# One pool of five PSUM banks in a two-block transformer kernel, and the order of work that comes with it

## The reference, cut to what matters

```
# layer 0: 16 heads of 16, tanh-GELU MLP of 1024
g1, g2, s1, s2, h1, h2 = silu(c) @ Wada.T + bada           # per sequence
a = ln(x) * (s1 + 1) + h1
q, k, v = a @ Wqkv.T + bias
q = q / |q| * scale ;  k = k / |k|                          # per head
x = x + (softmax(q k^T + mask) v @ Wproj.T + bproj) * g1
h = gelu((ln(x) * (s2 + 1) + h2) @ Wfc1.T + bfc1)
x = x + (h @ Wfc2.T + bfc2) * g2
# layer 1: 8 query heads of 32 with one key/value head, rotary positions, gated MLP of 1024
a = rms(x) * w1 * (1 + c @ tw1.T)
q, k, v = a @ Wq.T, a @ Wk.T, a @ Wv.T ; rope(q), rope(k)
x = x + softmax(q k^T / sqrt(32)) v @ Wo.T
b = rms(x) * w2 * (1 + c @ tw2.T)
x = x + (silu(b @ Wg.T) * (b @ Wu.T)) @ Wd.T
```

## Time and profile before

| | us |
|---|---|
| median of 3 runs (325.44 to 325.73) | 325.62 |
| the profiled execution | 326.22 |
| its span in the trace | 324.3 |
| PE busy in it | 297.7 |
| DVE busy | 221.0 |
| ACT busy | 205.8 |
| POOL busy | 155.5 |

### The profile page before, as it was taken

How to read it: one execution, slowest core, us unless ns; L and a number is a source line. 1 busy time by engine, 2 the same in 40 slices (tenths; PEclk the granted TensorE clock), 3 DMA queues, 4 the chain that set the end, 5 groups by cost and what they waited for, 6 DMA issues and landing times.

```text
span 324.3 us, 7219 instructions
## 1 busy us (share of the span) xinstructions
PE 297.7 (92%) x2458; PEld 250.5 (77%) x2458; DVE 221.0 (68%) x535; ACT 205.8 (63%) x698; POOL 155.5 (48%) x289
## 2 busy tenths in 40 slices
PE   6999789899879889977998999999999999999986
PEld 6979567668757667756787787889878988898975
DVE  4864996799885797799768567774748863661431
ACT  3553799999987797885899845448654535531210
POOL 3728885778947725895423453642246231320000
PEclk9596987999999999999999999999999999999999
DMA  6997622020000100000000100000000000000000
GB/s 184 250 299 246 217 83 80 32 68 3 0 2 0 68 0 3 3 1 2 0 2 14 55 0 2 0 17 2 18 1 2 0 18 16 3 0 19 16 2 32
DMA packets 14035, 14.28 MB, mean 44 GB/s; under 512 B 1568, under 2 KB 12960, under 8 KB 14000
## 3 DMA queue, kind: packets, MB, share of 16 engines
q1 hardware_dynamic: 14000, 13.83, 14.0%
HBM read 12.76 MB, written 1.06 MB: 43 GB/s over the span
## 4 chain that ended last, share of the span: by engine, by line
PE 64%; DVE 18%; POOL 8%; issue 5%; ACT 2%; DMA 1%; SPq 1%; DVEq 0%; POOLq 0%; ACTq 0%
PE ps_linear L1572 16%; PE ps_hidden L1376 6%; PE ps_hidden L1378 6%; PE ps_hidden L1377 6%; PE ps_probs L1507 5%; DVE z L1264 3%; PE ps_linear L1542 3%; PE ps_output L1523 3%; DVE neg_max L1275 3%; PE ps_scores L1496 2%; PE ps_hidden L1396 2%; PE ps_scores L1406 2%; PE ps_linear L1376 2%; PE ps_scores L1491 2%; PE ps_turn L1412 2%
## 5 line engine op out<-in xcount | busy, mean ns | idle before, releaser
L986 ACT ACTIVATE z<-z,neg_max 128x128 f32<-128x128 f32 x128 | 49.6, 395 | 4.0 <-DVE neg_max L1275 4.0
L826 POOL TENSOR_TENSOR h_lo<-xn,h_hi 128x256 fp32r<-128x256 f32 x32 | 25.0, 783 | 36.7 <-ACT h_hi L950 36.6
L1006 ACT ACTIVATE probsT<-ps_probs 128x512 f32<-128x512 f32 x48 | 28.4, 591 | 16.9 <-PE ps_probs L1507 14.5
L1507 PE MATMUL ps_probs<-ident,z 128*128 128x128 f32 x192 | 30.9, 285 | 3.7 <-ACT probsT L1006 2.3
L1042 ACT ACTIVATE g_a<-ps_hidden 128x256 f32<-128x256 f32 x32 | 12.4, 386 | 32.1 <-PE ps_hidden L1378 31.0
L1572 PE MATMUL ps_linear<-WdT,g_h 128*128 128x256 f32 x128 | 29.4, 383 | 1.3 <-DVE g_h L1347 1.3
L1572 PE MATMUL ps_linear<-Wfc2T,g_h 128*128 128x256 f32 x128 | 29.3, 382 | 1.3 <-DVE g_h L1334 0.8
L880 POOL TENSOR_TENSOR z<-z,row_inv 128x512 f32<-128x512 f32 x16 | 17.1, 1067 | 27.8 <-DVE row_inv L1289 27.7
L1507 PEld LDWEIGHTS ps_probs<-ident,z 128*128 128x128 f32 x192 | 21.6, 142 | 8.0 <-ACT probsT L1006 3.4
L1572 PEld LDWEIGHTS ps_linear<-Wfc2T,g_h 128*128 128x128 f32 x128 | 23.7, 190 | 4.9 <-issue 1.1
L1572 PEld LDWEIGHTS ps_linear<-WdT,g_h 128*128 128x128 f32 x128 | 23.7, 190 | 4.8 <-issue 1.4
(11 more groups left out here) (171 smaller groups left out, 910.7 us busy)
## 6 DMA issues: line engine op xcount, KB each, us to landing
gamma<-gamma_scratch SPq DMA_DIRECT2D x8, 256.0 KB, 3.5
stage<-in_Wada SPq DMA_DIRECT2D x6, 256.0 KB, 4.9
X<-in_x SPq DMA_DIRECT2D x4, 256.0 KB, 3.8
stage<-in_Wqkv SPq DMA_DIRECT2D x4, 256.0 KB, 5.6
Wfc2T<-in_Wfc SPq DMA_DIRECT2D x1, 1024.0 KB, 7.1
stage<-in_Wfc SPq DMA_DIRECT2D x4, 256.0 KB, 3.6
WdT<-in_Wd SPq DMA_DIRECT2D x1, 1024.0 KB, 8.0
stage<-in_Wg SPq DMA_DIRECT2D x4, 256.0 KB, 2.6
```

What stands on the lines that cost most here:

```text
L826: pool.tensor_tensor(h_lo[:, m, :, j * P:(j + 1) * P], h_full[:, m, j, :, :], h_hi[:, m, :, j * P:(j + 1) * P].bitcast(F32), ALU.subtract) ...
L986: ins = act.activation(z[:, d, u, :], z[:, d, u, :], ACT.Exp, bias=neg_max[:, d, u:u + 1], accum_out=head_sum[:, n % 2, t, u, b:b + 1])
L1006: act.activation(probsT[:, G % 2, :, :], bank_of(key)[:, :].rearrange("p (u q) -> p u q", u=4), ACT.Copy).then_inc(is_freed(key)[0], 1)
L1507: ins = pe.transpose(bank[:, u * P:(u + 1) * P], z[:, G % DEEP, u, :], ident[:, :])
```

## The change

The banks `turn`, `linear`, `hidden0`, `hidden1` and `probs` become `shared0` to `shared4`, one list. A step of any of those kinds takes the first bank of that list, and an emptied bank goes to its end. `scores` and `output` stay as they are. The number of banks is the same. Four assumed durations on DVE and POOL are set anew, and so are all the due times. No computation is added, removed or changed; the same steps run on the same engines in another order.

```
--- before.py
+++ after.py
 SLOT, START, DUE_US = 0.0, 0.0, 0.0
-GROUP_US = [-6.5, -554.0]
-ATT_BASE = [-3890.5, -875.0, -147.0, -2073.0, 1326.5, -859.0, 551.0, 1266.0]
+GROUP_US = [121.5, -772.0]
+ATT_BASE = [-4249.5, -1246.0, -1017.5, -1082.5, 2161.5, -634.0, -415.5, 75.0]
...
-BANK_KINDS = {"turn": ["turn"], "linear": ["linear"], "hidden": ["hidden0", "hidden1"],
-              "scores": ["scores"], "probs": ["probs"], "output": ["output"]}
+BANK_KINDS = {"shared": ["shared0", "shared1", "shared2", "shared3", "shared4"], "scores": ["scores"],
+              "output": ["output"]}
 BANKS = [b for kind in BANK_KINDS.values() for b in kind]
+KIND_OF = {b: kind for kind, banks in BANK_KINDS.items() for b in banks}
...
-                + [("modulated", c) for c in mods], "turn", at=a)
+                + [("modulated", c) for c in mods], "shared", at=a)
...
-                add(("qk_sum", n), "DVE", 1.3, [("qk_square", n), ("head_exp",), last_j.get(("qk", j))], at=a)
-                add(("qk_root", n), "Pool", 3.5, [("qk_sum", n)], at=a)
-                add(("qk_scale", n), "DVE", 1.0, [("qk_root", n)], at=a)
+                add(("qk_sum", n), "DVE", 1.45, [("qk_square", n), ("head_exp",), last_j.get(("qk", j))], at=a)
+                add(("qk_root", n), "Pool", 3.3, [("qk_sum", n)], at=a)
+                add(("qk_scale", n), "DVE", 0.75, [("qk_root", n)], at=a)
...
-                add(("qk_low", n), "Pool", 1.75, [("qk_high", n)], at=a)
-                add(("q_turn", n), "PE", 0.53, [("qk_low", n), last_scores], "turn", at=a)
+                add(("qk_low", n), "Pool", 1.9, [("qk_high", n)], at=a)
+                add(("q_turn", n), "PE", 0.53, [("qk_low", n), last_scores], "shared", at=a)
...
-                free[b.rstrip("01")].append(b)
+                free[KIND_OF[b]].append(b)
```

More of the change, by code:

```diff
@@ L89 @@
-MLP_SPAN = [-1198.5, 1936.5]
+    'Wfc1': 1874.5, 'Wg': 7279.0, 'Wkv': 1646.0, 'Wq': 6943.5, 'Wqkv': 3242.5, 'Wu': -1435.0, 'ada': 2378.0,
+    'tw1': -52.5, 'tw2': -1582.0}
+MLP_SPAN = [-1696.5, 2329.0]
 SHIFT = {
-    'warm': 900.0, 'angles': -2187.5, 'attn_copy': 408.5, 'cond_silu': 2646.0, 'cond_tanh': 268.5, 'down':
-    1119.0, 'exp': 3337.0, 'fc1': -2109.0, 'gamma_load': -3710.0, 'gamma_store': 470.5, 'gate': 868.5,
-    'gate_up': 2067.0, 'gelu': -2310.0, 'gelu_in': 1778.5, 'gelu_inner': 2225.5, 'head_clip': -1104.0,
-    'head_exp': 166.0, 'inv_copy': 1919.0, 'inv_spread': 370.0, 'inv_turn': -492.5, 'k_copy': 120.0,
-    'k_turn': 698.5, 'load': -1753.5, 'load_small': -943.0, 'load_whole': 1820.0, 'load_x': -2746.5,
-    'mask_add': -1389.5, 'modulate': 4259.0, 'modulated': -3996.0, 'norm_apply': -4120.5, 'norm_high':
-    -993.0, 'norm_low': 3131.5, 'norm_mod': 1463.0, 'norm_probs': -802.5, 'norm_root': 7283.0, 'norm_stats':
-    -4034.5, 'norm_turn': 224.0, 'probs_copy': -1014.5, 'probs_turn': -1171.5, 'project': 1292.5, 'q_copy':
-    -741.0, 'q_turn': 2729.5, 'qk1_copy': 3677.0, 'qk1_turn': -4022.0, 'qk_copy': -1291.0, 'qk_high':
-    -2900.0, 'qk_low': 125.0, 'qk_product': -5390.5, 'qk_root': 3053.0, 'qk_scale': 9.0, 'qk_square':
-    -5621.0, 'qk_sum': 3071.0, 'qkv1_copy': -2594.0, 'qkv1_product': 2597.5, 'residual': -1863.5,
-    'residual_add': 1116.5, 'rope': 946.5, 'row_inverse': 2355.0, 'row_max': -2133.0, 'scores': -2490.5,
-    'sines': 3241.0, 'store': 4877.5, 'sum_inverse': -3013.0, 'tanh': 1284.0, 'v_copy': -4072.0,
-    'v_product': 494.0, 'values': -394.5, 'weight_high': -803.0, 'weight_low': 253.0, ('norm_stats', 'a'):
-    670.5, ('norm_stats', 'm'): -860.0, ('norm_root', 'a'): -1654.5, ('norm_root', 'm'): -537.5,
-    ('norm_apply', 'a'): -2512.5, ('norm_apply', 'm'): -1353.0, ('norm_turn', 'a'): -2523.0, ('norm_turn',
[3 rows of a table removed]
@@ new lines @@
+    'warm': 900.0, 'angles': -1693.5, 'attn_copy': 49.5, 'cond_silu': 3308.0, 'cond_tanh': -705.5, 'down':
+    1008.0, 'exp': 3066.0, 'fc1': -2574.5, 'gamma_load': -4400.5, 'gamma_store': 879.0, 'gate': 1003.5,
+    'gate_up': 2508.0, 'gelu': -3373.0, 'gelu_in': 2190.0, 'gelu_inner': 2416.5, 'head_clip': -1027.5,
+    'head_exp': 545.5, 'inv_copy': 2058.0, 'inv_spread': 114.0, 'inv_turn': -805.0, 'k_copy': 675.0,
+    'k_turn': 22.5, 'load': -1932.5, 'load_small': -1475.0, 'load_whole': 2426.0, 'load_x': -2586.0,
@@ new lines @@
+    'mask_add': -1510.5, 'modulate': 4124.0, 'modulated': -4692.5, 'norm_apply': -4689.5, 'norm_high':
+    -610.5, 'norm_low': 2029.0, 'norm_mod': 1981.0, 'norm_probs': -1525.0, 'norm_root': 8105.5,
+    'norm_stats': -4674.0, 'norm_turn': 1064.5, 'probs_copy': -2148.0, 'probs_turn': -960.0, 'project':
+    1602.5, 'q_copy': -1509.0, 'q_turn': 2124.5, 'qk1_copy': 4152.5, 'qk1_turn': -5779.5, 'qk_copy':
+    -1796.0, 'qk_high': -3549.0, 'qk_low': -1451.5, 'qk_product': -5840.5, 'qk_root': 3194.5, 'qk_scale':
@@ new lines @@
+    -1337.5, 'qk_square': -5096.5, 'qk_sum': 2915.5, 'qkv1_copy': -2268.5, 'qkv1_product': 3030.0,
+    'residual': -2489.0, 'residual_add': 1769.5, 'rope': 1548.0, 'row_inverse': 3100.0, 'row_max': -2835.0,
+    'scores': -1207.0, 'sines': 4246.5, 'store': 6611.0, 'sum_inverse': -3437.5, 'tanh': 2231.5, 'v_copy':
+    -4961.0, 'v_product': 733.0, 'values': -205.0, 'weight_high': 963.0, 'weight_low': 311.0, ('norm_stats',
+    'a'): 352.0, ('norm_stats', 'm'): -888.5, ('norm_root', 'a'): -798.0, ('norm_root', 'm'): -1397.5,
@@ L112, in CHUNK_DUE @@
+    ('norm_apply', 'a'): -2897.5, ('norm_apply', 'm'): -1281.0, ('norm_turn', 'a'): -2964.5, ('norm_turn',
[3 rows of a table added]
 def CHUNK_DUE(c):
@@ L243, in list_steps @@
                 w_ready = ("weight_low", CHUNK_AT[("Wqkv", 2)])
-                add(("qk_product", n), "PE", 1.55, [("norm_low", "a", n), w_ready, last_j.get(("qk", j))], "linear", at=a)
+                add(("qk_product", n), "PE", 1.55, [("norm_low", "a", n), w_ready, last_j.get(("qk", j))], "shared", at=a)
                 add(("qk_copy", n), "DVE", 0.6, [("qk_product", n), ("load_small",), last_j.get(("qk", j))], frees=("qk_product", n),
```

24 lines of the change are left out of this document (11 added, 13 removed), and 6 rows, old and new, of the table SHIFT.

## The result

The changed kernel takes 327.54 us (324.78 to 331.03, 20 runs) against 325.1 us (323.76 to 326.65, 20 runs) for the kernel before on the same chip: ratio 1.0064, interval 1.0041 to 1.0088. Forecast were 316.1 us and a range up to 324.0. The result lies where the forecast had put a chance of 0.12.

What follows compares the result with a forecast made beforehand. TensorE was the engine to watch: full from 180 to 261.2 us, ACT nearly full before 96, waits ruling between. Terms -4.9 - 2.0 - 2.6 - 2.0 - 1.2 + 1.5 + 1.0 + 0.7 = -9.5 took 325.62 to 316.1 us, range 310.5 to 324.

Steps and rivals of the forecast that it cites:

- (a): From 96 to 180 us, PE's waits for banks that the pool frees vanish: -4.9 us.
- (b): From 36.77 to 96 us: 1.2 for POOL's weight split going behind `qk_low` of sequence 4, 0.8 for `k_turn`'s bank wait: -2.0 us.
- (c): Some 17 us of PE work moved ahead of sequence 8's first scores fills half the idle time left: -2.6 us.
- (f): Ahead of the first scores of sequence 8, 14 more fillers, half their time counted as cost: +1.5 us.
- (g): Five tight places in the new order, where a step gets a bank not yet emptied, cause new waits: +1.0 us.
- (h): Round 2's eight DVE steps run longer beside POOL's `qk_root` and `qk_low` of sequences 8 and 9: +0.7 us.
- (d): From the first scores of sequence 8 to those of sequence 14, nine fillers go: -2.0 us.
- (e): At the end, `values` and a `project` replace fillers while `down` waits for the last gated tile: -1.2 us.
- The rival that the waits only change their name: Steps freed from a bank wait then wait for data that comes no sooner: 322.7 us, chance 0.13.
- The rival in which TensorE runs dry in the second half: Work taken forward leaves PE idle between first scores of sequences 8 and 14, costing 11.0 us: 329.1 us, chance 0.11.
- the bound of 164.5: Sign that the forecast is wrong: first scores of sequence 8 after 164.5 us, 147.5 plus 17 us of moved work.
- the rival's mechanism: The granted clock falls twice more as fillers go where PE could wait anew, costing 6.8 us: 322.9 us, chance 0.05.

Runs made afterwards that it cites:

- e3: The kernel before with its order unchanged on every engine, only the banks dealt from the pool of five: 323.23 us, ratio 0.9944.
- e8: The kernel before with its old kinds of banks, every engine's order from 60 us on newly searched by a sum of durations: 315.12 us, ratio 0.9693.
- e5: The changed kernel with the low parts of the last five weight chunks set to zero on POOL instead of subtracted: 324.01 us, ratio 0.9969.
- e6: The changed kernel with POOL's MLP residual of sequences 2 and 3 on one column instead of 256: 324.03 us, ratio 0.9971.
- e11: The changed kernel with both POOL cuts, constant low parts of five weight chunks and one-column residuals of sequences 2 and 3: 321.77 us, ratio 0.9893.
- e4: The changed kernel with 24 more fillers at four places ahead of PE's long waits: 326.19 us, ratio 1.0049.

## Why the forecast was wrong

By stage, the steps ahead of the first scores of sequence 8, (a) + (b) + (c) + (f) + (g) + (h), were to give -6.3 us and gave +6.9; (d) + (e), -3.2, gave -7.3. That is 9.1 of the 11.4 us. The other 2.3 are as much as the median of the changed kernel lies above its profiled execution, a distance that goes with the granted clock.

- (a) and the bank part of (b), -5.7: the failed step, the one on which the forecast stood. The rows named banks, the pool freed them, and e3 is worth 1.8 us. What I credited as won was a wait for the latest of two inputs, and the other, the data, came next to it: from 60 us on 8.3 us of bank waits turned into 7.6 of data waits. The rival that the waits only change their name had the right mechanism. But it isn't a law: in e8's order the same edit is worth 5.0.
- (b), the weight behind `qk_low`: as forecast, `qk_low` of sequence 4 starts 2.4 us sooner (80.4 against 82.8). It bought nothing, for I followed the chain only to POOL; three chunks of the weights, split at 76.5, 81.6 and 97.0 us before, now stand together at 90 us, where DVE had to stand still beside them (X), and the first scores came 3.5 us later.
- (c), -2.6: the work was there, but it didn't reach the waits: from sequence 4 to 8, with some 17 us of PE work more, the slack grew by 4.3 us.
- (d) -2.0 and (e) -1.2: right in direction, too small, -5.0 and -2.3, with the 1.0 us wait for the last gated tile as foreseen. The rival in which TensorE runs dry in the second half is refuted: 90.02 of 92.10 us busy. From the first scores of sequence 8 to the end it is 95.7%, though, where I had expected over 97.
- (f), +1.5: mis-sized. In that stage the fillers went from 3.3 to 8.6 us. I took them as covering waits that were there; they stood for longer ones. The first scores of sequence 8 at 170.2 us passed the bound of 164.5 that I had set.
- (g), +1.0: right, about 1 us of bank waits is left.
- (h), +0.7 with a bound of 7.7: mis-sized, and looked for at the wrong place. I priced `gelu` beside `qk_root`; there the eight DVE steps of round 2 take 0.68 to 0.81 us, so the bound of 7.7 priced the wrong side. What counted were `norm_apply` and `gelu` beside the weights (e5: 3.5 us) and POOL's own queue ahead of the norms, in part stretched by the same exclusion (e6: 3.5 us), 5.8 us together (e11). These runs take POOL's work away as well, so the 5.8 us are the worth of the two places; the exclusion is at most that. The Trainium skill (SBUF — State Buffer, Who interferes with whom) says that such instructions exclude each other and that the order of issue decides which one waits. The trace agrees: where `gelu_inner` (L1326) started first, it was POOL that took longer, 0.73 us for its usual 0.25.

```profile
156.92 0.69 DVE L1326 SCALAR_TENSOR_TENSOR g_a<-g_a,g_u 128x512 f32<-128x512 f32 x1
156.98 0.73 POOL L843 TENSOR_TENSOR qk_t<-qk_t,qk_u 128x32 f32<-128x32 f32 x1
```

- The clock: the rival's mechanism came true at a smaller size. Two falls of 3.4 us at the half level are 3.4 us of work, not 6.8, in the profiled execution; the falls followed the waits. By the 20 executions the lower clock of the usual one goes with 2.3 us. No run takes the clock alone away: e4 won 1.35 us at most, with fillers that take time themselves.

The runs name 3.9 (a, b: 5.7 credited, 1.8 measured) + 5.1 (X and Y: 5.8 less the 0.7 of (h)) = 9.0 us, and e4 up to 1.35 more. With the 4.1 that (d) and (e) gave beyond the forecast, 15.5 had to be explained; 5 to 6.5 us are named by no single run and stay open, and the 2.3 that go with the clock are among them.

## What to carry to other kernels

- Count idle time and fillers together, by stage. A change that only moves this sum gives little, however many waits vanish; here it was 36.7 us before, 36.3 in the changed kernel, 36.7 in e3, and 15 to 17 in the orders with the pool that gained 5 to 6%.
- Look whether a profiled execution is a usual one before two traces are compared: one of the slower ones before and one of the quicker ones behind hid the whole loss here.
- A wait for a buffer is worth what the next latest input leaves of it. Look up when that input arrives before the wait is credited, and follow moved work to where it lands, on its own engine and on the one that it excludes.
- Try a resource change on the old order first, then let the order use it.
